# An attention and mixture-of-experts kernel: the exponentials' biases of the even heads are made by GpSimd instead of VectorE

## The reference

```python
q = _fq_sym(q * scale, axis=-1)       # 16 heads of 32, int8 steps
k = _fq_sym(k, axis=-1)
v = _fq_sym(v, axis=2)
attn = jnp.einsum('bhqd,bhkd->bhqk', q, k)
attn = jax.nn.softmax(attn.astype(jnp.float32), axis=-1)
attn = _fq_unsigned(attn, axis=-1)    # max / 255 is one step
out = jnp.einsum('bhqk,bhkd->bhqd', attn, v)
x = x + out @ Wp + bp                 # then layernorm, router, experts
```

## Time and profile before

| | |
|---|---|
| median of 3 runs | 726.53 us (724.64 to 728.48) |
| the profiled execution | 725.01 us, its span 723.2 us |
| mean granted TensorE clock | 0.986 of full speed |
| busy, share of the span | PE 86%, DVE 79%, ACT 64%, POOL 56% |

### The profile page before, as it was taken

The page is one execution under the profiler, slowest core; times in us unless marked ns, Lnnn a source line. Parts: engine busy times, 40 slices in busy tenths (PEclk is TensorE's granted clock), DMA queues, the critical chain, the costliest instruction groups (busy, mean ns, idle before and its releaser), DMA issues.

```text
span 723.2 us, 15795 instructions
## 1 busy us (share of the span) xinstructions
PE 618.9 (86%) x5307; PEld 328.3 (45%) x5307; DVE 567.9 (79%) x926; ACT 462.1 (64%) x559; POOL 402.8 (56%) x455
## 2 busy tenths in 40 slices
PE   6999999666867777777777688799999999999995
PEld 3444444233434333443434356455555555555543
DVE  4998888999999999999999998783646547465430
ACT  6344459789979989898989898343434334344321
POOL 5255458537587878787877874234334453344503
PEclk9999999999999999999999999899999999999998
DMA  7777857999989999999999999269697787967914
GB/s 254 198 148 176 182 135 145 182 190 194 173 165 198 184 198 193 188 192 189 189 189 185 200 176 170 88 213 212 162 253 161 225 221 176 242 157 225 145 27 58
DMA packets 318516, 129.42 MB, mean 179 GB/s; under 512 B 293508, under 2 KB 293508, under 8 KB 318472
## 3 DMA queue, kind: packets, MB, share of 16 engines
q1 hardware_dynamic: 311296, 112.64, 72.8%
q0 software_dynamic: 7168, 16.26, 11.0%
q10 hardware_dynamic: 8, 0.01, 0.0%
HBM read 44.33 MB, written 12.06 MB: 78 GB/s over the span
## 4 chain that ended last, share of the span: by engine, by line
PE 46%; issue 14%; DVE 11%; POOL 8%; DMA 7%; ACT 7%; SPq 5%; POOLq 1%; another core or an unknown queue 0%; ACTq 0%; DVEq 0%
PE psum L1668 43%; DMA work<-work 7%; ACT work L1065 4%; DVE spare L1400 3%; POOL work L672 3%; DVE spare L1391 2%; SPq L483 2%; SPq L481 2%; POOL exp_bias L678 1%; PE psum L1987 1%; SPq L450 1%; ACT work L967 1%; POOL work L657 1%; POOL bias_hl L636 1%; POOL out_dram L846 1%
## 5 line engine op out<-in xcount | busy, mean ns | idle before, releaser
L1065 ACT ACTIVATE work<-spare,exp_bias 128x2048 uint8<-128x2048 f32 (+1 forms) x127 | 253.2, 1995 | 29.3 <-POOL exp_bias L678 21.8
L1400 DVE TENSOR_SCALAR_CACHE_REDUCE spare<-psum,q_step_now 128x1024 f32<-128x1024 f32 x128 | 162.8, 1279 | 2.7 <-PE psum L1839 2.5
L672 POOL CAST work<-work 128x2048 int16<-128x2048 uint8 x70 | 132.3, 1890 | 39.2 <-DMA work<-work 35.4
L1391 DVE TENSOR_SCALAR_CACHE_REDUCE spare<-psum,q_step_now 128x2048 f32<-128x2048 f32 x64 | 150.6, 2353 | 0.1
L1839 PE MATMUL psum<-keys_region,work 128*128 128x512 f16 x256 | 73.1, 385 | 43.0 <-DVE spare L1400 27.1
L834 POOL DMA_INDIRECT work<-x_rows,slot_tok x32 | 49.8, 1558 | 88.5 <-DVE slot_w L1600 75.1
L1839 PE MATMUL psum<-keys_region,bias_hl 128*128 128x512 f16 x256 | 70.6, 381 | 28.4 <-DVE spare L1400 22.9
L846 POOL DMA_INDIRECT out_dram<-keys_region,slot_tok x32 | 51.7, 1615 | 74.8 <-ACT keys_region L1160 67.8
L1798 PEld LDWEIGHTS psum<-values_region,work 128*128 128x128 f16 x2016 | 65.0, 96 | 36.5 <-POOL work L672 21.6
L1668 PE MATMUL psum<-work,spare 128*128 128x480 f16 (+1 forms) x396 | 80.5, 364 | 0.0
L1798 PE MATMUL psum<-values_region,work 128*128 128x32 f16 x2016 | 70.0, 177 | 10.8 <-POOL work L672 7.0
(11 more groups left out here) (250 smaller groups left out, 1005.4 us busy)
## 6 DMA issues: line engine op xcount, KB each, us to landing
spare<-in_L_ffn_Wd_dram SPq DMA_DIRECT2D x8, 1024.0 KB, 15.5
spare<-in_L_ffn_Wg_dram SPq DMA_DIRECT2D x7, 1024.0 KB
spare<-in_L_ffn_Wu_dram SPq DMA_DIRECT2D x7, 1024.0 KB, 10.3
work<-in_ctx_dram SPq DMA_DIRECT2D x3, 1024.0 KB, 5.8
work<-work SPq DMA_TRANSPOSE x174, 3.7
token_region<-in_L_xattn_Wkv_dram SPq DMA_DIRECT2D x2, 1024.0 KB, 6.1
resid<-in_x_dram SPq DMA_DIRECT2D x2, 1024.0 KB, 8.9
out_dram<-work SPq DMA_DIRECT2D x8, 256.0 KB, 2.6
```

What stands on the lines that cost most here:

```text
L672: nc.gpsimd.tensor_copy(p_T_int[h % 4], pair_bytes[h % 4]).then_inc(unpacked, 1)
L1065: nc.scalar.activation(p_out, scores, ACT.Exp, bias=exp_bias[:, h % 4:h % 4 + 1], scale=-1.0, accum_out=p_sum[:, h:h + 1]).then_inc(exp_do ...
L1391: nc.vector.tensor_scalar(staged[h % 4], psum[:, at:at + 4, :].rearrange("p b k -> p (b k)"), q_step_now[:, h:h + 1], None, ALU.mult, ALU.min,
L1400: nc.vector.tensor_scalar(staged[h % 4][:, 1024 * c:1024 * c + 1024], psum[:, at:at + 2, :].rearrange("p b k -> p (b k)"), q_step_now[:, h ...
```

## The change

GpSimd makes the biases of the even heads too, in tiles 1 to 6 all eight and in tile 7 those of heads 0 to 12. It is a simpler instruction than that of the odd heads, one addition of a constant to one column. It stands at the head of its step in GpSimd's list: at h = 2, for example, ahead of `deviation_begun`. VectorE's instruction between the two halves goes away there. It still makes all of tile 0, and heads 14 and 15 of tile 7. ScalarE then waits on `bias_made` where it waited on `edge_bias`.

```diff
@@ gpsimd: make_bias(i, h)
-                nc.gpsimd.tensor_scalar(exp_bias[:, at], s_low[:, at], s_first[:, at], LN255, ALU.min, ALU.add).then_inc(bias_made, 1)
+                if h % 2:
+                    nc.gpsimd.tensor_scalar(exp_bias[:, at], s_low[:, at], s_first[:, at], LN255, ALU.min, ALU.add).then_inc(bias_made, 1)
+                else:
+                    nc.gpsimd.tensor_scalar(exp_bias[:, at], s_low[:, at], LN255, None, ALU.add).then_inc(bias_made, 1)
@@ gpsimd: attention_tile
                 for h in range(H if following else H - 2):
-                    if h % 2:
-                        make_bias(i, h)
+                    make_bias(i, h)
@@ scalar: attention_tile
-                    elif h % 2 and (following or not after_rows or h < H - 1):
-                        act.wait_ge(bias_made, HQ * i - HQ + h // 2 + 1)
+                    elif following or h < H - 2:
+                        act.wait_ge(bias_made, H * i - H + h + 1)
                     else:
-                        act.wait_ge(edge_bias, H + HQ * i - HQ + (h + 1) // 2 + 1)
+                        act.wait_ge(edge_bias, h + 3)
@@ vector: attention_tile
-                    if h or not first:
+                    if first and h or last and h == H - 2:
                         make_bias(i, h)
```

More of the change, by code:

```diff
@@ L1411, in make_bias, with attention_tile @@
                     nc.vector.tensor_scalar(exp_bias[:, at], s_low[:, at], LN255, None, ALU.add).then_inc(edge_bias, 1)
-            def attention_tile(i, first, after_first=False):
+            def attention_tile(i, first, after_first=False, last=False):
                 for h in range(0, H, 2):
@@ L1437, in _ @@
                 attention_tile(i, False)
-            attention_tile(QT - 1, False)
+            attention_tile(QT - 1, False, last=True)
             make_bias(QT - 1, H - 1)
```

## The result

The changed kernel takes 733.34 us (median of 6 runs, 729.30 to 735.64) where the kernel before took 725.67 us (6 runs, 722.48 to 728.48): a ratio of 1.0119, 95% interval 1.0091 to 1.0147, or +8.6 us (the two medians alone differ by 7.7, a quotient of 1.0106). The profiled execution took 732.79 us, with a span of 731.1. The change made the kernel slower, as forecast (732.7, that is +6.2). Part of the closeness is luck: over these 6 runs the median of the kernel before lies 0.9 us under the 726.53 that the forecast started from, so the change cost 1.5 to 2.4 us more than forecast while the end figure is 0.6 off. Executions much slower than the others of their kernel (2985 us in e_chain, 1213 in e_short_after, 735.40 in v_split, 734.38 in one series of the kernel before) are left out of the ratios in this document.

What follows compares the result with a forecast made beforehand. GpSimd's round of 38.42 us a tile was taken to set the attention's pace. Tiles 2 to 6 +6.1, tile 7 +0.8, tile 1 -0.4 gave +6.5, leaned to +6.2 on 726.5: 732.7 us, range 726 to 737.5.

Steps and rivals of the forecast that it cites:

- GpSimd's list sets the pace, not VectorE: Attention tiles: GpSimd's round takes 38.42 us, longer than VectorE's 37.9, so GpSimd sets the pace.
- The walk: Reading GpSimd's list through tile 4 for outside waits: none at h = 0 to 3, 0.48 and 0.82 us at h = 9 and 12.
- The removed instructions are worth 0.07 us each: VectorE, between half stagings: 0.56 us a tile, 3.9 for all 55, counted only in tile 1 as -0.4 us.
- Each added instruction: GpSimd's list: an even bias lasts 0.19 to 0.30 us and adds 0.43 at h = 6 and h = 14.
- The sum for a round: GpSimd's list in a loop tile: +1.22 us, from 38.42 to about 39.64, bounds 0.9 to 1.7.
- Whatever lengthens GpSimd's list in h = 0 to 7 or 13 to 15 lengthens it: GpSimd's round: additions there lengthen the round; only h = 8 to 12 has 1.30 us to give.
- Even biases just in time: ScalarE's exponentials of heads 8 and 10: biases ready at 304.7 and 309.5, wanted at 305.14 and 309.73.
- the second rival: Even biases late for ScalarE too, no cover at h = 8 to 12: round 2.4 us longer, +14, 740; chance 0.10.
- The sum in the attention: Tiles 1 to 7: 6.1 us in tiles 2 to 6, 0.8 in tile 7, -0.4 in tile 1, together +6.5.
- The lean to 6.2: Whole forecast: +6.5 lowered to +6.2 us, since a wait often partly swallows small extra work in such a round.
- After the attention nothing changes.: Behind the attention: the last exponentials and the products behind them shift as a whole, with no further change.
- VectorE sets the pace after all: Attention tiles: rival in which tiles become 0.56 us shorter, 726.5 - 3.9 = 722.6 us; chance 0.14.

Runs made afterwards that it cites:

- e_chain: Against the kernel before, GpSimd makes the biases of the odd heads and of heads 0, 2, 6 and 14, VectorE the others: ratio 1.0122.
- e_short_after: The changed kernel with one Newton step left out, GpSimd's list 1.08 us shorter: ratio 1.0090 against the kernel before.
- v_split: Against the kernel before, GpSimd makes biases of odd heads but 15, and of 0, 4, 8, 10, 12; VectorE the others: ratio 1.0020.
- e_dummy: The kernel before with eight more constant additions per tile on GpSimd, whose result nobody reads: ratio 1.0136.
- e_none: Against the kernel before, VectorE makes all biases, GpSimd none: ratio 1.0084.
- e_swap: Against the kernel before, exchanged: GpSimd makes the biases of the even heads, VectorE those of the odd heads: ratio 1.0034.
- e_short_before: The kernel before with one Newton step left out, GpSimd's list 1.08 us shorter: ratio 0.9998.
- e_cover: Against the kernel before, GpSimd makes the biases of the odd heads and of heads 4, 8, 10 and 12, VectorE the others: ratio 1.0051.
- e_late_cover: Against the kernel before, tile 1 unchanged; from tile 2 on GpSimd makes biases of odd heads and of 4, 8, 10, 12: ratio 1.0050.

## Why the prediction was right

- **GpSimd's list sets the pace, not VectorE.** Shown for the changed kernel by e_dummy (VectorE keeps its work, the loss is there), and by e_none, in which VectorE does set it and its tiles come at an even 39.04. For the kernel before it holds by little: with the list shortened its round went from 38.5 only to 38.24, close to VectorE's 38.12. The walk rests on no outside wait in h = 0 to 3, and the earlier trace rows show one of 0.37 us, put down to VectorE; but GpSimd stands idle the same 0.37 us ahead of that bias in tiles 2, 5 and 6, where its own L694 is named, so it is rightly counted as list.
- **The removed instructions are worth 0.07 us each.** The half stagings now start 1.21 and 1.20 us apart, where the first took 1.27. Whole tiles say the same: e_none has eight even biases more on VectorE than e_swap, and 39.04 - 38.55 = 0.49 us, 0.06 each. The odd ones are dearer: with VectorE at its own pace, eight of them in addition take 39.04 - 38.12 = 0.92 us a tile (e_none against e_short_before), 0.12 each. Both are below the fixed cost of about 150 cycles, an estimated 0.156 us, that the Trainium skill gives for an operation on SBUF (VectorE: DVE Perf Modes, section on the TRN2 errata). The duration of the instruction agrees with that figure (L1411 before: 0.156 us in the mean of 64); what it adds from start to start, under the next staging, is less, and there the measurement decides. As the gain from the even ones lay on an engine that waits, nothing of it was seen; VectorE waits 2.0 us a tile, as forecast. But the forecast named the exponentials as what it would wait for, and that step was wrong in its path: only 0.5 us of the 9.8 are that. The wait comes through TensorE, whose products wait for unpacked probabilities and hold up the scores behind them. The end of the path was right, its middle not.
- **Each added instruction.** It takes 0.22 us (0.19 to 0.30 allowed), and 0.42 and 0.43 at heads 14 and 6, as walked.
- **The sum for a round**, +1.22, measured +1.15. One term was mis-sized, and another put at nothing, in a way that partly cancels. h = 0 to 4 was put at 0.36 and is 0.31; h = 14 at 0.43 and is 0.42. But h = 6 was put at its full 0.43, with h = 8 to 12 at nothing: together they cost 0.12 + 0.16 = 0.28. The step that failed is "Whatever lengthens GpSimd's list in h = 0 to 7 or 13 to 15 lengthens it". Head 6's step also stands in front of the 0.48 us wait at h = 9, and can use it. e_short_after and e_short_before show why: that stretch is set by a path over ScalarE and the transposes, of 10.05 and 10.04 us. e_chain and e_cover alone could not show it.
- **Even biases just in time** for heads 8 and 10, late at 0, 2 and 6: so in the trace. Late biases were the second rival. They are not needed for the loss (e_dummy), but they are not nothing: on the path above, head 6 waits 0.17 us for its own. In the changed kernel list and path are of nearly equal length (9.99 and 10.05 us for the stretch), so that shortening one alone there brings little. No run has the full list with only the late biases mended and nothing added to VectorE, so their share is argued and not measured.
- **The sum in the attention**, +6.5 before leaning, measured +6.1 and +7.2 in the two pairs of profiles. The lean to 6.2 was not needed; the timed +7.7 to +8.6 lies above both.
- **"After the attention nothing changes."** Neither shown nor refuted: the two profiles of the changed kernel differ there by 5 us (286.2 and 281.2), so that 1 or 2 us of the change would not be seen.
- **VectorE sets the pace after all** (the faster rival): it would have needed a round below 38.4; it was 39.5.

What stays open: the timed differences are mostly larger than those at the attention's end, by 0 to 2.2 us (8.6 against 6.6 for the changed kernel, 3.6 against 1.6 for e_late_cover, 0 against -2.0 for e_short_before). Part may be that the kernel before has the stretched instruction, or a lowered granted clock behind the attention, less often than others; two profiles of it can't say. Nor is it settled why a new split costs extra in its first tiles.

## What to carry to other kernels

An engine that is busy 56% of the time can be the one that sets the pace: look for the list that has no outside wait from one round to the next, and price an added instruction from start to start (0.43 us here), not by its duration (0.22). A wait in that list is cover: an instruction added ahead of it, as far back as the point at which the waited-for work branched off, can use it up, and each piece of cover can be spent only once. When work is traded between two lists of nearly equal length (38.1 and 38.4 us here), there is little to win in either direction: measure the longer list with idle instructions first.

## What the hardware showed that I had not expected

In 10 of the 14 profiles one VectorE instruction on a 128x1 column took 1.55 to 1.89 us instead of 0.16 to 0.22; it started within half a microsecond of the end of the last exponential. It was not the same instruction each time, and the kernel before as well as the changed one shows it in one of two profiles. In all 10, the first gather of the expert stage started 22.0 to 23.9 us after the last exponential, in the other four 20.2 to 20.7. The whole time behind the attention does not follow it alone (284.5 us without it and 284.4 with it in the kernel before), since the granted clock behind the gather, 0.84 to 1.00 over 20 us in the four profiles above, differs between executions of one kernel as well. What decides either is not in the program's code and stays open. A single profile cannot tell a change of 3 us there.
